# An attention kernel: the weighing of two quarters in one place, and waits at the quarter that needs them

## The chip, the cores and the metric

The kernel runs on one core of one Trainium2 chip. The metric is the device time of the whole program in microseconds. A core has a matrix engine (TensorE, "PE" in the profile; its weight loads are "PEld"), VectorE ("DVE"), ScalarE ("ACT"), GpSimd ("POOL") and SyncE ("SP"), which here only issues DMA. Each runs its own instructions in order and waits for the others by semaphores.

## What is computed

A transformer block over 2 batches of 2048 tokens with 512 features, 16 heads of 32, followed by a rotation of the features. The part that the change touches is the attention:

```python
scores = einsum('bhqd,bhkd->bhqk', q / sqrt(32), k) + attention_bias   # bias: 2 x 16 x 2048 x 2048
scores = where(src_mask, -inf, scores)
probs = softmax(scores, axis=-1)
ctx = einsum('bhqk,bhkd->bhqd', probs, v)
```

Ahead of it stand a layer norm with modulation and the projections to q, k and v; behind it the output projection, a second layer norm, a GELU feed-forward of 2048 and the rotation. All is in 32-bit floats; the bias alone is 512 MB that is read once.

## The kernel before

Three phases run one after the other: projections, attention (`phase_b`), and output projection with feed-forward. Attention goes over 64 trips (a head and half of a batch's queries) of 8 tiles of 128 queries each, so 512 tiles. A tile is 128 queries by 2048 keys; its bias lies in one of the 8 slots of `ring`. Four tiles (`QT`) make a unit of 512 queries; 128 units in all, two to a trip, and `probT` has room for two.

A tile i passes the engines like this:

- SyncE loads the bias into `ring[j]` as soon as the tile 8 before it has been turned in full (line 543); GpSimd adds the mask's penalty to it (line 572).
- TensorE computes the scores in two halves of 1024 keys (`score`, c = 0 and 1, two matmuls of 512 keys each), and adds the penalty of the last 192 keys with one more matmul (line 721).
- VectorE adds scores and bias of each half, writes the sum back to the ring and keeps the running minimum of the negated sum (`add`, line 636). The second half starts from the minimum of the first (`low_part`), and so waits on VectorE's own counter `added` (line 631).
- ScalarE takes the exponential of the whole tile (line 668), in the next step.
- TensorE turns the tile two steps after its scores: four quarters (`turn`, n = 0 to 3), each of four transposes of 128x128 into one PSUM bank (line 749). There are three banks for this; `turn_bank` gives the quarters the banks 0, 1, 2, 0 in even tiles and 2, 1, 0, 2 in odd ones. So a quarter can be turned only when the one before it in that bank has been copied out.
- ScalarE copies quarters 0 and 1 to `probT` (line 678, counter `out_act`), VectorE quarters 2 and 3 (line 620, counter `out_dve`).
- TensorE weighs the values of a whole unit with `probT` (`weigh`, line 772): for each quarter four matmuls of 32 columns side by side, which sum in `bank_ctx` over the four quarters. The profile counts each of them twice, since it goes through the array in two passes.

The order of each engine within a step is written out by hand. TensorE: scores of half 0 and half 1, quarters 0 and 1, one quarter of the weighing, quarters 2 and 3. The four quarters of a unit's weighing thus fall to four steps in a row. The waits for free banks stand earlier than their quarters: the one for the exponential ahead of the last score matmul of half 0 and the one for quarter 2 of the tile before ahead of the last of half 1 (`free_before_turn`), others in the middle of a quarter (c = 2). VectorE: add 0, copy of quarter 3 of the tile three steps back, add 1, copy of quarter 2 of the tile two steps back. ScalarE: exponential, copies of quarters 0 and 1, in some steps a copy of `bank_ctx`.

Even and odd steps are those with even and odd j, the place of the tile in its trip.

## Time and profile before

| | |
|---|---|
| median of 3 runs | 3553.28 us (3551.06 to 3555.66) |
| the profiled execution | 3553.73 us, its span 3552.1 us |
| mean granted clock of TensorE | 0.984 |
| TensorE matmul busy | 3418.1 us, 96% |
| VectorE busy | 2482.1 us, 70% |
| GpSimd busy | 2074.7 us, 58% |
| ScalarE busy | 1885.3 us, 53% |
| memory traffic | 906.14 MB, 255 GB/s over the span |

The page cuts the span into 40 slices. In those of the attention phase TensorE, VectorE and DMA all stand at 9 tenths or more and ScalarE at 8; in the others TensorE alone does. A busy share is therefore to be read in the attention phase alone: there three engines are nearly full, and which of them sets the pace is seen only from the order in which they wait for each other. In the rows, an instruction's start is measured and the end of a matmul is modelled; matmuls overlap in the array, so the distance from start to start is what one costs. The count behind a row says how many like instructions it merges.

### The profile page before, as it was taken

How to read it: one execution, taken by the hardware profiler on the slowest of the kernel's cores; microseconds unless marked ns; L12 is line 12 of the kernel's file. 1: busy time of each engine (PE TensorE's matmuls, PEld its weight loads, DVE VectorE, ACT ScalarE, POOL GpSimd, SP SyncE). 2: the span in 40 equal slices, each digit the busy share in tenths (PEclk: the TensorE clock that was granted, in tenths of full speed). 3: DMA queues.
4: the chain of work that ended last, by engine and by line, in shares of the span. 5: the costliest groups of instructions: out<-in, count | busy, mean ns of one | idle time of the engine just before them, and what ended most of it. 6: DMA issues, size and time to landing. Idle time of an engine off the chain costs nothing. (4 is left out here: it accounts for less than half of the span.)

```text
span 3552.1 us, 61044 instructions
## 1 busy us (share of the span) xinstructions
PE 3418.1 (96%) x18338; PEld 1942.0 (55%) x18338; DVE 2482.1 (70%) x4177; ACT 1885.3 (53%) x2538; POOL 2074.7 (58%) x642
## 2 busy tenths in 40 slices
PE   8999799999999999999999999994899999999997
PEld 3444466666666666666666666662344444444443
DVE  5665599999999999999999999993334333343332
ACT  3222388888888888888888888883111111111110
POOL 0000599999899998999998999992202201210100
PEclk9999899999999999999999999997899999999999
DMA  8999999999999999999999999996302211220100
GB/s 290 336 338 340 363 360 348 351 345 345 397 350 349 350 345 365 380 350 346 347 349 385 360 349 347 347 349 207 89 8 63 71 28 43 71 56 15 47 12 12
DMA packets 290234, 906.14 MB, mean 255 GB/s; under 512 B 93344, under 2 KB 93344, under 8 KB 213408
## 3 DMA queue, kind: packets, MB, share of 16 engines
q1 hardware_dynamic: 237584, 803.04, 63.1%
q10 hardware_dynamic: 50064, 94.39, 7.6%
q0 software_dynamic: 2560, 8.39, 0.7%
q8 instruction: 13, 0.21, 0.0%
q14 instruction: 13, 0.11, 0.0%
HBM read 763.12 MB, written 142.61 MB: 255 GB/s over the span
## 5 line engine op out<-in xcount | busy, mean ns | idle before, releaser
L572 POOL TENSOR_TENSOR ring<-ring,penb 128x1856 f32<-128x1856 f32 x512 | 1904.3, 3752 | 503.9 <-DMA penb<-pen_scratch 417.1
L668 ACT ACTIVATE ring<-ring,low 128x2048 f32<-128x2048 f32 x512 | 1028.6, 2009 | 319.2 <-DVE low L636 319.2
L749 PEld LDWEIGHTS b_T<-ident,ring 128*128 128x128 f32 x8192 | 889.3, 141 | 431.1 <-DVE probT L620 427.8
L749 PE MATMUL b_T<-ident,ring 128*128 128x128 f32 x8192 | 1090.8, 276 | 3.7 <-DVE probT L620 3.7
L636 DVE CUSTOM_DVE_ANT_0 ring<-scores,ring 128x1024 f32<-128x1024 f32 x512 | 627.2, 1225 | 177.6 <-PE scores L715 153.8
L620 DVE COPY probT<-b_T 128x512 f32<-128x512 f32 x1024 | 702.3, 686 | 4.5 <-PE b_T L749 4.5
L636 DVE CUSTOM_DVE_ANT_0 ring<-scores,ring,low_part 128x1024 f32<-128x1024 f32 x512 | 652.8, 1275 | 0.4
L715 PE MATMUL scores<-keys,queries 128*128 (+1 forms) x2048 | 621.8, 425 | 21.3 <-DMA queries<-q_rows 16.9
L772 PE MATMUL bank_ctx<-probT,values 128*32 128x512 f32 x4096 | 544.9, 604 | 0.0
L678 ACT COPY probT<-b_T 128x512 f32<-128x512 f32 x1024 | 537.8, 575 | 2.0 <-PE b_T L749 2.0
L939 POOL TENSOR_TENSOR y_out<-rot_a,rot_b 128x512 f32<-128x512 f32 x32 | 40.5, 1266 | 787.3 <-DVE rot_b L1097 787.3
L991 ACT ACTIVATE gate<-c_up,b_scaled 128x512 f32<-128x512 f32 x128 | 87.9, 687 | 741.1 <-PE c_up L1148 741.0
L1148 PE MATMUL c_up<-hT,w 128*128 (+1 forms) x1024 | 460.8, 594 | 0.7 <-ACT hT L983 0.7
L1158 PE MATMUL c_acc<-w,hidden 128*128 128x512 f32 x1024 | 458.9, 592 | 0.0
L715 PEld LDWEIGHTS scores<-keys,queries 128*128 128x128 f32 x2048 | 347.1, 190 | 144.1 <-DVE probT L620 74.3
L1078 DVE SCALAR_TENSOR_TENSOR hidden<-c_up,b_col,gate 128x512 f32<-128x512 f32 x128 | 96.0, 750 | 396.2 <-ACT gate L991 377.6
L1158 PEld LDWEIGHTS c_acc<-w,hidden 128*128 128x128 f32 x1024 | 194.0, 190 | 241.5 <-issue 241.5
L1148 PEld LDWEIGHTS c_up<-hT,w 128*128 128x128 f32 x1024 | 191.3, 191 | 223.1 <-issue 222.1
L932 POOL TENSOR_TENSOR parts<-parts 128x1024 f32<-128x1024 f32 x30 | 70.8, 2360 | 161.4 <-DMA parts<-ctx_scratch 161.0
L1129 PE MATMUL c_fore<-wo,ctxT 128*128 128x512 f32 x256 | 117.3, 603 | 19.0 <-DVE ctxT L1031 19.0
L721 PE MATMUL scores<-penb,identb 128*128 128x192 bf16 x512 | 131.7, 257 | 0.0
L772 PEld LDWEIGHTS bank_ctx<-probT,values 128*32 128x32 f32 x4096 | 80.8, 108 | 86.9 <-issue 86.6
(102 smaller groups left out, 1738.9 us busy)
## 6 DMA issues: line engine op xcount, KB each, us to landing
ring<-in_fside_Bx16xSxS SPq DMA_DIRECT2D x512, 1024.0 KB, 7.5
keys<-k_rows SPq DMA_DIRECT2D x64, 1024.0 KB, 8.5
values<-v_heads ACTq DMA_DIRECT2D x128, 256.0 KB, 6.5
queries<-q_rows SPq DMA_DIRECT2D x128, 256.0 KB, 8.1
ctx_scratch<-ctxp ACTq DMA_DIRECT2D x128, 256.0 KB, 6.8
parts<-ctx_scratch SPq DMA_DIRECT2D x128, 256.0 KB, 4.9
k_rows<-part_hi SPq DMA_DIRECT2D x64, 256.0 KB, 3.3
k_rows<-part_lo SPq DMA_DIRECT2D x64, 256.0 KB, 3.6
```

The source lines that it names most:

```text
L572: nc.gpsimd.tensor_tensor(ring[:, j, 0:POOL_MASKED], ring[:, j, 0:POOL_MASKED], penb[:, j, 0:POOL_MASKED], ALU.add).then_inc(masked, 1)
L620: nc.vector.tensor_copy(probT[:, hh, QR * n:QR * (n + 1), q * P:(q + 1) * P], turn_bank(k, n)[:].rearrange("p (c q) -> p c q", c=QR)).then ...
L636: nc.vector.tensor_tensor_reduce(out=at, in0=scores[c][:], in1=at, scale=-1.0, scalar=low_part[:, j:j + 1] if c else -MASKED, op0=ALU.add, ...
L668: nc.scalar.activation(ring[:, k, :], ring[:, k, :], ACT.Exp, bias=low[:, k:k + 1], scale=-1.0, accum_out=column(sums_all, trip, k)).then_ ...
L678: nc.scalar.copy(probT[:, hh, QR * n:QR * (n + 1), q * P:(q + 1) * P], turn_bank(k, n)[:].rearrange("p (c q) -> p c q", c=QR)).then_inc(ou ...
L715: last = nc.tensor.matmul(scores[c][:, n * N:(n + 1) * N], queries[:, hh, q * P:(q + 1) * P], keys[:, bass.ds(it % 2, 1), c * CW + n * N:c ...
L721: last = nc.tensor.matmul(scores[c][:, CW - PE_MASKED:CW], identb[:], penb[:, j, POOL_MASKED:S], start=False, stop=True)
L749: last = nc.tensor.transpose(turn_bank(slot, n)[:, c * P:(c + 1) * P], ring[:, slot, at:at + P], ident[:])
L772: last = nc.tensor.matmul(bank_ctx[DH * c:DH * (c + 1), :], values[:, hh, QR * n + c, :], probT[:, hh, QR * n + c, :], start=(n == 0), sto ...
L1129: last = nc.tensor.matmul(fore[t % 2][:], ctxT[:, c, t * P:(t + 1) * P], wo[:, c, :], start=(c == 0), stop=(c == DB - 1))
L1148: last = nc.tensor.matmul(up[f % 2][:], w1[:, c, f * P:(f + 1) * P], hT[:, bass.ds(u % 2, 1), c, :].rearrange("p o n -> p (o n)"), start=( ...
L1158: last = nc.tensor.matmul(acc[t][:], hidden[:, k % 4, t * P:(t + 1) * P], w2[:, k, :], start=(k == 0), stop=(k == FB - 1))
```

## The change

Four things are changed, all in `phase_b`:

- `weigh` runs in even steps alone, between the third and the fourth quarter, and takes two quarters of the unit (0 and 1 where j is 2 or 6, 2 and 3 where j is 0 or 4), sixteen passes in place of eight.
- TensorE's waits stand directly ahead of what needs them: exponential and the copy of the tile before's quarter 2 at quarter 0, that of quarter 1 at quarter 1, that of quarter 3 at quarter 2, that of this tile's quarter 0 at quarter 3; those of the weighing at the weighing.
- VectorE copies quarter 3 in the same step as quarter 2, so that its order is add 0, add 1, copy of quarter 2, copy of quarter 3.
- ScalarE's step is cut into functions; the order of its instructions stays.

```diff
--- before.py
+++ after.py
@@ -608,9 +608,9 @@
         def _(dve):
             nc.vector.tensor_copy(identb[:], ident[:]).then_inc(identb_ready, 1)
 
-            def copy_quarter(it, j, n, lag):
-
-                t, k = it * R + j - lag, (j - lag) % R
+            def copy_quarter(it, j, n):
+
+                t, k = it * R + j - 2, (j - 2) % R
                 hh, q = k // QT, k % QT
                 if live(t, NT):
                     dve.wait_ge(turned, TURNED0 + t * 4 + n + 1)
@@ -640,9 +640,9 @@
 
             def step(it, j):
                 add(it, j, 0)
-                copy_quarter(it, j, 3, 3)
                 add(it, j, 1)
-                copy_quarter(it, j, 2, 2)
+                copy_quarter(it, j, 2)
+                copy_quarter(it, j, 3)
 
             trips(dve, step)
 
@@ -657,7 +657,8 @@
             load_values(0, 0)
             load_values(0, 1)
 
-            def step(it, j):
+            def exponentials(it, j):
+
                 i = it * R + j
                 if live(i - 1, NT):
                     k, trip = (j - 1) % R, it if j else it - 1
@@ -667,16 +668,23 @@
                         nc.scalar.copy(low_all[:, bass.ds(trip, 1), :].rearrange("p o n -> p (o n)"), low[:]).then_inc(low_kept, 1)
                     nc.scalar.activation(ring[:, k, :], ring[:, k, :], ACT.Exp, bias=low[:, k:k + 1], scale=-1.0,
                                          accum_out=column(sums_all, trip, k)).then_inc(exp_done, 1)
+
+            def copy_quarter(it, j, n):
+                i = it * R + j
                 if live(i - 2, NT):
                     k = (j - 2) % R
                     hh, q = k // QT, k % QT
-                    for n in (0, 1):
-                        act.wait_ge(turned, TURNED0 + (i - 2) * 4 + n + 1)
-                        if q == 0 and n == 0:
-
-                            act.wait_ge(pv_done, PV0 - 1 + (it * 2 if j == 2 else it * 2 + 1))
-                        nc.scalar.copy(probT[:, hh, QR * n:QR * (n + 1), q * P:(q + 1) * P],
-                                       turn_bank(k, n)[:].rearrange("p (c q) -> p c q", c=QR)).then_inc(out_act, 1)
+                    act.wait_ge(turned, TURNED0 + (i - 2) * 4 + n + 1)
+                    if q == 0 and n == 0:
+
+                        act.wait_ge(pv_done, PV0 - 1 + (it * 2 if j == 2 else it * 2 + 1))
+                    nc.scalar.copy(probT[:, hh, QR * n:QR * (n + 1), q * P:(q + 1) * P],
+                                   turn_bank(k, n)[:].rearrange("p (c q) -> p c q", c=QR)).then_inc(out_act, 1)
+
+            def step(it, j):
+                exponentials(it, j)
+                copy_quarter(it, j, 0)
+                copy_quarter(it, j, 1)
                 unit, hh = closing(it, j), 0 if j < QT else 1
                 if j % QT == 1 and live(unit, UNITS):
                     act.wait_ge(pv_done, PV0 + unit + 1)
@@ -709,8 +717,6 @@
                         pe.wait_ge(q_in[hh], it * 16 + 16)
                     need(pe, added, i * CH + c - 1)
                 for n in range(CW // N):
-                    if n == CW // N - 1:
-                        free_before_turn(it, j, c)
                     if live(i, NT):
                         last = nc.tensor.matmul(scores[c][:, n * N:(n + 1) * N], queries[:, hh, q * P:(q + 1) * P],
                                                 keys[:, bass.ds(it % 2, 1), c * CW + n * N:c * CW + (n + 1) * N].rearrange("p o n -> p (o n)"),
@@ -722,66 +728,57 @@
                                                 start=False, stop=True)
                     last.then_inc(scored, 1)
 
-            def free_before_turn(it, j, c):
-
-                t = it * R + j - 2
+            def turn(it, j, n):
+
+                t, slot = it * R + j - 2, (j - 2) % R
                 if live(t, NT):
-                    if c == 0:
+                    if n == 0:
                         pe.wait_ge(exp_done, t + 1)
-                    else:
                         need(pe, out_dve, t * 2 - 1)
-
-            def turn(it, j, n):
-
-                t, slot = it * R + j - 2, (j - 2) % R
-                if n == 2 and live(t, NT):
-                    need(pe, out_dve, t * 2)
-                for c in range(QR):
-                    if c == 2:
-                        if n == 0 and live(t, NT):
-                            need(pe, out_act, t * 2)
-                        if n == 1:
-                            copied_before_weigh(it, j)
-                        if n == 2 and live(t, NT):
-                            pe.wait_ge(out_act, t * 2 + 1)
-                    if live(t, NT):
+                    if n == 1:
+                        need(pe, out_act, t * 2)
+                    if n == 2:
+                        need(pe, out_dve, t * 2)
+                    if n == 3:
+                        pe.wait_ge(out_act, t * 2 + 1)
+                    for c in range(QR):
                         at = (QR * n + c) * P
                         last = nc.tensor.transpose(turn_bank(slot, n)[:, c * P:(c + 1) * P], ring[:, slot, at:at + P], ident[:])
-                if live(t, NT):
                     last.then_inc(turned, 1)
 
             def weighed(it, j):
+
                 unit = it * 2 - 2 if j < 2 else it * 2 - 1 if j < 6 else it * 2
-                return (j - 2) % QT, unit, 1 if 2 <= j < 6 else 0
+                return unit, 1 if 2 <= j < 6 else 0, 0 if j % QT == 2 else 2
 
             def copied_before_weigh(it, j):
 
-                n, unit, hh = weighed(it, j)
+                unit, hh, n = weighed(it, j)
                 if live(unit, UNITS):
-                    pe.wait_ge(out_act if n < 2 else out_dve, (unit * QT + QT - 1) * 2 + n % 2 + 1)
+                    if n == 0:
+                        pe.wait_ge(v_in[hh], it * 16 if j == 2 else it * 16 + 16)
+                        need(pe, ctx_copied, unit)
+                    pe.wait_ge(out_act if n == 0 else out_dve, (unit * QT + QT) * 2)
 
             def weigh(it, j):
 
-
-                n, unit, hh = weighed(it, j)
-                if live(unit, UNITS) and n == 0:
-                    pe.wait_ge(v_in[hh], it * 16 if j == 2 else it * 16 + 16)
-                    need(pe, ctx_copied, unit)
-                for c in range(4):
-                    if live(unit, UNITS):
-                        last = nc.tensor.matmul(bank_ctx[DH * c:DH * (c + 1), :], values[:, hh, QR * n + c, :],
-                                                probT[:, hh, QR * n + c, :], start=(n == 0), stop=(n == 3))
-                if live(unit, UNITS) and n == 3:
+                copied_before_weigh(it, j)
+                unit, hh, first = weighed(it, j)
+                for n in (first, first + 1):
+                    for c in range(4):
+                        if live(unit, UNITS):
+                            last = nc.tensor.matmul(bank_ctx[DH * c:DH * (c + 1), :], values[:, hh, QR * n + c, :],
+                                                    probT[:, hh, QR * n + c, :], start=(n == 0), stop=(n == 3))
+                if live(unit, UNITS) and first == 2:
                     last.then_inc(pv_done, 1)
 
             def step(it, j):
                 score(it, j, 0)
                 score(it, j, 1)
-                turn(it, j, 0)
-                turn(it, j, 1)
-                weigh(it, j)
-                turn(it, j, 2)
-                turn(it, j, 3)
+                for n in range(4):
+                    if n == 3 and j % 2 == 0:
+                        weigh(it, j)
+                    turn(it, j, n)
 
             trips(pe, step)
```

## Rows read from the trace of the kernel before

**Rows 1.** Page, part 1: busy us (share of the span) and instructions.

```profile
PE 3418.1 (96%) x18338; PEld 1942.0 (55%) x18338; DVE 2482.1 (70%) x4177; ACT 1885.3 (53%) x2538; POOL 2074.7 (58%) x642
```

**Rows 2.** Windows, one stretch of the attention phase; columns named in line one.

```profile
core 0: us, PE busy (x) PEld busy (x) DVE busy (x) ACT busy (x) POOL busy (x), PEclk, DMA share, GB/s
...
1500.00:1900.00 400.00, 400.00 (x2938) 258.25 (x2935) 368.40 (x607) 324.92 (x443) 378.38 (x102) 1.00 0.95 347
```

**Rows 3.** Timeline of TensorE, a step: start us, us, engine line op tiles xcount.

```profile
1501.05 0.27 PE L749 MATMUL b_T<-ident,ring 128*128 128x128 f32 x1
1501.08 1.20 PE L715 MATMUL scores<-keys,queries 128*128 x4
...
1502.13 0.26 PE L721 MATMUL scores<-penb,identb 128*128 128x192 bf16 x1
...
1502.22 1.04 PE L749 MATMUL b_T<-ident,ring 128*128 128x128 f32 x8
...
1503.18 1.06 PE L772 MATMUL bank_ctx<-probT,values 128*32 128x512 f32 x8
...
1504.18 1.09 PE L749 MATMUL b_T<-ident,ring 128*128 128x128 f32 x8
...
1505.03 1.27 PE L715 MATMUL scores<-keys,queries 128*128 x4
```

**Rows 4.** Timeline of TensorE in cuts that split the groups of rows 3.

```profile
1501.40 0.40 PE L715 MATMUL scores<-keys,queries 128*128 x1
...
1503.64 0.61 PE L772 MATMUL bank_ctx<-probT,values 128*32 128x512 f32 x4
...
1504.35 0.38 PE L749 MATMUL b_T<-ident,ring 128*128 128x128 f32 x2
```

**Rows 5.** Timeline of VectorE, the same step.

```profile
1502.03 1.23 DVE L636 CUSTOM_DVE_ANT_0 ring<-scores,ring 128x1024 f32<-128x1024 f32 x1 [0.30 <-PE scores L715]
...
1503.18 0.69 DVE L620 COPY probT<-b_T 128x512 f32<-128x512 f32 x1
1503.78 1.27 DVE L636 CUSTOM_DVE_ANT_0 ring<-scores,ring,low_part 128x1024 f32<-128x1024 f32 x1
...
1504.98 0.69 DVE L620 COPY probT<-b_T 128x512 f32<-128x512 f32 x1
```

**Rows 6.** Timeline, a copy of VectorE and TensorE's weight load that waits for it.

```profile
1501.04 0.69 DVE L620 COPY probT<-b_T 128x512 f32<-128x512 f32 x1
...
1501.78 0.19 PEld L715 LDWEIGHTS scores<-keys,queries 128*128 128x128 f32 x1 [0.20 <-DVE probT L620]
```

**Rows 7.** Timeline of GpSimd, four tiles in a row.

```profile
1600.29 14.90 POOL L572 TENSOR_TENSOR ring<-ring,penb 128x1856 f32<-128x1856 f32 x4 [0.19 <-DMA ring<-in_fside_Bx16xSxS]
```

**Rows 8.** Timeline of VectorE in the phase's first steps, without copies between adds.

```profile
397.76 1.28 DVE L636 CUSTOM_DVE_ANT_0 ring<-scores,ring,low_part 128x1024 f32<-128x1024 f32 x1
...
402.62 1.23 DVE L636 CUSTOM_DVE_ANT_0 ring<-scores,ring 128x1024 f32<-128x1024 f32 x1 [3.56 <-issue]
...
403.98 1.28 DVE L636 CUSTOM_DVE_ANT_0 ring<-scores,ring,low_part 128x1024 f32<-128x1024 f32 x1
...
407.76 1.28 DVE L636 CUSTOM_DVE_ANT_0 ring<-scores,ring,low_part 128x1024 f32<-128x1024 f32 x1
...
408.97 0.69 DVE L620 COPY probT<-b_T 128x512 f32<-128x512 f32 x1
```

**Rows 9.** Timeline at the phase's end: two copies, then transposes behind a wait.

```profile
2421.96 1.28 DVE L620 COPY probT<-b_T 128x512 f32<-128x512 f32 x2
...
2422.76 0.31 PEld L749 LDWEIGHTS b_T<-ident,ring 128*128 128x128 f32 x3 [0.77 <-issue]
...
2422.93 0.49 PE L749 MATMUL b_T<-ident,ring 128*128 128x128 f32 x3
```

**Rows 10.** Timeline of ScalarE, the exponential of the same step.

```profile
1501.24 2.01 ACT L668 ACTIVATE ring<-ring,low 128x2048 f32<-128x2048 f32 x1 [0.89 <-DVE low L636]
```

**Rows 11.** Timeline of TensorE in the first steps: scores that wait for add 1.

```profile
399.11 1.22 PE L715 MATMUL scores<-keys,queries 128*128 128x512 f32 x2 [0.20 <-DVE low L636]
```

More of the change, by code:

```diff
@@ L723, in score @@
                     last.then_inc(scored, 1)
-            def free_before_turn(it, j, c):
-                t = it * R + j - 2
-                if live(t, NT):
-                    if c == 0:
-                        pe.wait_ge(exp_done, t + 1)
-                    else:
-                        need(pe, out_dve, t * 2 - 1)
             def turn(it, j, n):
                 t, slot = it * R + j - 2, (j - 2) % R
-                if n == 2 and live(t, NT):
-                    need(pe, out_dve, t * 2)
-                for c in range(QR):
-                    if c == 2:
-                        if n == 0 and live(t, NT):
-                            need(pe, out_act, t * 2)
-                        if n == 1:
-                            copied_before_weigh(it, j)
-                        if n == 2 and live(t, NT):
-                            pe.wait_ge(out_act, t * 2 + 1)
-                    if live(t, NT):
+                if live(t, NT):
+                    if n == 0:
+                        pe.wait_ge(exp_done, t + 1)
+                        need(pe, out_dve, t * 2 - 1)
+                    if n == 1:
[5 more added lines that the diff above has]
+                    for c in range(QR):
                         at = (QR * n + c) * P
                         last = nc.tensor.transpose(turn_bank(slot, n)[:, c * P:(c + 1) * P], ring[:, slot, at:at + P], ident[:])
-                if live(t, NT):
                     last.then_inc(turned, 1)
```

## The prediction

> **What bounds the kernel now.** I read the page's busy shares first: TensorE 96%, VectorE 70% [rows 1]. These are means over three phases; the change touches only the attention phase of 512 steps. So next the busy time of a stretch inside it [rows 2]: in 400 us TensorE is busy all of the time at granted clock 1.00, and it ran 2938 matmuls. A step has 29 (4 scores, 1 mask, 16 transposes, 8 of weighing), so a step lasts 400 / (2938 / 29) = 3.948 us. Times 512 that is 2021 us of the 3552.1.
>
> The timeline of TensorE shows what the 3.95 us are [rows 3, 4]. Scores start at 1501.08, the mask at 1502.13, eight transposes at 1502.22, weighing at 1503.18, eight transposes at 1504.18, the next scores at 1505.03. Transposes are 0.109 us apart (from 1504.35 to 1505.03 are six of them and 0.03 us of hand-over). From the last transpose to the weighing are 0.96 - 7 x 0.109 = 0.20 us, where the next transpose would have come after 0.11. A weighing pass (four matmuls side by side) lasts 1503.64 - 1503.18 = 0.46 us; the second one is followed by the first transpose after 0.60 (1504.35 - 0.11 - 1503.64). So entering and leaving the weighing costs 0.09 + 0.14 = 0.23 to 0.24 us, once a step. Nothing of it is idle beyond that: TensorE is the bound.
>
> VectorE is close behind [rows 5]: add 0 at 1502.03, copy 1.15 later, add 1 another 0.60 later, copy another 1.20 later, then 0.69 of copy and 0.30 of waiting for the scores. Its work alone is 1.15 + 0.60 + 1.20 + 0.60 = 3.55 us a step. The weight load of the last score matmul already waits for the copy that started at 1501.04 [rows 6]; the matmul itself is late by at most 0.02. GpSimd needs 14.90 / 4 = 3.72 a tile and waits for DMA in between [rows 7]. So the step could not fall below 3.72 in any case.
>
> **The change part by part.**
>
> *Weighing two quarters at once, in even steps.* The matmuls stay. One entry and one exit of two go: TensorE's own work for two steps falls from 7.90 to 7.66 us. But an odd step is now 3.95 - 1.15 = 2.80 us of it and an even one 4.86. A weighing of two quarters lasts 0.20 + 3 x 0.46 + 0.60 = 2.18 us from the last transpose of the third quarter to the first of the fourth [rows 3, 4].
>
> *VectorE: the copy between the adds goes behind them.* Add 1 takes its running minimum from add 0 and waits for its completion. Now a copy covers that wait: add 0 to copy 1.15, copy to add 0.60 [rows 5]. Where no copy lies between them, in the first steps of the phase, add 1 starts 403.98 - 402.62 = 1.36 us after add 0, and the copy behind it 1.21 later [rows 8]. So the wait costs 0.21 us a step once its cover is gone. Two copies in a row are 0.60 apart: the row of two at 2421.96 is 1.28 long, one is 0.69 [rows 9, 5]. VectorE's work rises from 3.55 to 1.36 + 1.21 + 0.60 + 0.60 = 3.77 us. Alone that still fits under 3.95.
>
> The Trainium skill speaks against this price: "VectorE: DVE Perf Modes", section "The DRAIN you can't avoid", has a semaphore between chained operations cost nothing extra. The row shows 0.21 us for this pair, a form with an accumulator.
>
> *The fourth quarter's copy moves a step earlier, ahead of the next add 0.* Queued behind it on VectorE is now everything of the next step. In an even step the fourth quarter is turned only after the two-quarter weighing, so VectorE stands at this copy while TensorE weighs, and can't start add 0 the sooner for anything, since the next scores come behind the same transposes.
>
> *The waits stand at the quarter.* Satisfied waits cost nothing: the transposes with one inside a quarter are as far apart as the others. The wait for the third quarter's copy leaves the last score matmul (gain at most 0.02) and goes to the first transpose. What it costs there if it is late is shown at the phase's end [rows 9]: copies start at 2421.96, the second transpose behind the wait at 2422.93, so the first in effect at 2422.82, 0.86 after the start of the first copy. The lower bound is the older place: weight load 1501.78 after copy 1501.04 = 0.74 [rows 6]. I take 0.86, which is this very pair of waits with this very instruction behind it.
>
> *ScalarE* keeps its order (exponential, copies of quarters 0 and 1); it stands idle for 0.89 us ahead of each exponential [rows 10], so I cost it at nothing. If that cover went, the fourth quarter of odd steps would be late, and there TensorE has the half microsecond of slack that the sum below gives it. SyncE's loads of the ring still hang on the fourth quarter and GpSimd gets more time a tile than now, not less: nothing. The second weighing, and with it the release of the context bank, ends a step earlier than now, which nobody waits for.
>
> **The sum.** What decides is a round trip of two steps, from add 0 of an odd step to add 0 of the next odd step:
> - add 0 to add 1, 1.36; add 1 to the third quarter's copy, 1.21 [rows 8];
> - this copy to the first transpose of the even step, 0.86 [rows 9];
> - twelve transposes, start of first to start of last, 11 x 0.109 = 1.20; weighing 0.20 + 1.38 + 0.60 = 2.18; fourth quarter 3 x 0.109 = 0.33 [rows 3, 4];
> - last transpose at 1501.05 to second score matmul at 1501.40, 0.35; that to add 0 at 1502.03, 0.63 [rows 3 to 5].
> Together 8.12 us, 4.06 a step; with the passes at 0.454 and the other figures unrounded 8.09, or 4.045. All of it is in series: the copy can't start before add 1 is done, the quarter not before the copy, since they share a bank. TensorE needs 7.66 and VectorE 7.54 for the same two steps, so about 0.45 us of each pair is idle on TensorE. It would show in even steps, ahead of the second pair of scores, which waits for add 1 (0.4), and ahead of the first quarter (0.1).
>
> The change is then 4.045 - 3.948 = +0.097 us a step, times 512 = +50 us. To the profiled execution (span 3552.1, 3553.7 in all) that makes 3603; the median of the runs is 0.4 below it, so 3603 again; I say 3602, since what VectorE now and then waits for GpSimd can only shrink at a slower pace.
>
> Bounds: if the copy hands over in 0.74, the trip is 7.97; it can't be much less, as the second pair of scores needs add 1 as well: add 1 at 397.76 [rows 8], scores at 399.11 [rows 11], 1.35, then 0.23 + 0.26 + 0.09 to the first transpose, 1.93 against my 2.07. That is 3.985, or 3573. Upwards: each further quarter of the even step that finds its wait late, or just met, loads weights unhidden, about 0.06 from the load at 2422.76 to the transpose [rows 9]; two of them make 8.21, 4.105, or 3634.
>
> **The rivals.**
>
> *The forecast*, +0.097 a step: 0.70, from 3573 to 3625.
>
> *The round trip is hidden and TensorE stays the bound (faster).* Place: the hand-over at the first quarter of even steps. Price: two steps take TensorE's 7.66, 3.83 each, -0.118 x 512 = -60: 3493. It decides if the trip is 7.66 or less, so if 0.43 us of the sum above isn't in series. For it: TensorE is the bound today by a hair only, and entering and leaving is real work saved. Against it: every term has a row of its own, and the two terms that the change brings (0.21 of the self-wait, 0.92 of a second weighing behind the third quarter) can't lie elsewhere. 0.10.
>
> *The self-wait is free.* The same trip with 1.15 in place of 1.36 is 7.88, 3.94 a step, which is the present pace: 3550. For it would speak only that the rows of the first steps belong to a start in which VectorE waited for other things; but nothing in them is between the two adds. 0.05. It is the result that the skill's rule named above would give.
>
> *Further late waits (slower still).* TensorE's sequencer stands at the first quarter's wait and behind it has to compute and pass the waits of two quarters and three of the weighing. Place: the first to third quarter of even steps. Price: 0.12 us or more of a pair, 3625 to 3650. It decides if these take longer than the 1.3 us of twelve transposes. 0.12.
>
> *Nothing happens*, as the two costs and the gain cancel, or the instructions end up in the order of now: 3554, 0.03.
>
> **How the numbers follow.** The likeliest is 3602. From 3565 to 3640 lie nearly all of the forecast's 0.70 and most of the slower rival, together about 0.8; the faster rival, the two near 3550 and the far end are left out. A measurement of this kernel tells apart about 0.2%, 7 us. Faster by more: 0.11 (the faster rival and a little of the third). Within: 0.08. Slower: 0.81.
>
> **What would show it.** The two steps should differ: on TensorE first transpose to first transpose about 4.8 us from an even step to an odd one, 3.3 from an odd to an even. Add 0 to add 1 should be 1.36 in every step. VectorE should wait about 0.5 us for the fourth quarter in even steps and hardly elsewhere. The weighing should be a block of 16 matmuls and about 1.9 us, its entry and exit as now. The transposes of even steps should be released by VectorE's copy. If instead TensorE is busy without a gap and a pair of steps lasts 7.66, the sum was wrong in the hand-over; if add 0 to add 1 is 1.15, in the self-wait; if a pair is over 8.2, waits cost TensorE more than the end of the phase shows. A fall of the granted clock from 1.00 would break all of it; at this busy share I see none in the rows.

## The result and the profile after

The changed kernel takes 3589.95 us (median of 4 runs, 3588.65 to 3592.43), the kernel before 3552.17 beside it. The ratio is 1.0106, 95% interval 1.0088 to 1.0123: 38 us slower, where 50 were forecast. The profiled execution's span is 3587.0 us, against 3552.1. Line numbers have moved: the transposes are now L746 (L749 before), the scores L721 (L715), the mask L727 (L721), the weighing L770 (L772), ScalarE's copies L681 (L678) and its exponential L669 (L668); VectorE's lines are the same.

The page of the changed kernel, busy shares and VectorE's groups (busy us, mean ns | idle before, releaser), answers to [rows 1]:

```profile
PE 3413.2 (95%) x18338; PEld 1963.3 (55%) x18338; DVE 2517.2 (70%) x4177; ACT 1903.4 (53%) x2538; POOL 2073.9 (58%) x642
...
L620 DVE COPY probT<-b_T 128x512 f32<-128x512 f32 x1024 | 680.9, 686 | 92.1 <-PE b_T L746 92.1
...
L636 DVE CUSTOM_DVE_ANT_0 ring<-scores,ring,low_part 128x1024 f32<-128x1024 f32 x512 | 657.4, 1284 | 76.0 <-DVE low_part L636 11.0
```

TensorE's busy share went down by one point only. The groups say more: VectorE's copies, which waited for TensorE for 4.5 us in all, now do for 92.1 us, and add 1 has 76.0 us of idle time before it, part of it put down to VectorE itself (`low_part`). The stretch that answers to [rows 2]:

```profile
core 0: us, PE busy (x) PEld busy (x) DVE busy (x) ACT busy (x) POOL busy (x), PEclk, DMA share, GB/s
1500.00:1900.00 400.00, 391.74 (x2879) 256.64 (x2877) 368.24 (x597) 322.01 (x435) 371.87 (x101) 1.00 0.88 342
```

2879 matmuls in 400 us are 400 / (2879 / 29) = 4.029 us a step, against 3.948. TensorE still reads as 98% busy, because the end of a matmul is modelled and covers much of the gap behind it. DMA fell from 0.95 to 0.88, and the granted clock is 1.00 in both, so the clock is no cause. A pair of steps on TensorE, answering to [rows 3] (steps with weighing begin their transposes at 1501.68 and 1509.73, the one without at 1506.48):

```profile
1501.68 1.50 PE L746 MATMUL b_T<-ident,ring 128*128 128x128 f32 x12
...
1506.48 1.93 PE L746 MATMUL b_T<-ident,ring 128*128 128x128 f32 x16
1508.17 0.71 PE L721 MATMUL scores<-keys,queries 128*128 x2
1509.04 0.73 PE L721 MATMUL scores<-keys,queries 128*128 x2 [0.16 <-DVE low L636]
1509.61 0.26 PE L727 MATMUL scores<-penb,identb 128*128 128x192 bf16 x1
1509.73 1.50 PE L746 MATMUL b_T<-ident,ring 128*128 128x128 f32 x12
1511.17 1.92 PE L770 MATMUL bank_ctx<-probT,values 128*32 128x512 f32 x16
1513.02 0.66 PE L746 MATMUL b_T<-ident,ring 128*128 128x128 f32 x4
1513.43 1.18 PE L721 MATMUL scores<-keys,queries 128*128 x4
```

and in cuts, as [rows 4]:

```profile
1509.87 0.38 PE L746 MATMUL b_T<-ident,ring 128*128 128x128 f32 x2
...
1512.48 0.61 PE L770 MATMUL bank_ctx<-probT,values 128*32 128x512 f32 x4
...
1513.19 0.38 PE L746 MATMUL b_T<-ident,ring 128*128 128x128 f32 x2
```

From first transpose to first transpose are 4.80 and 3.25 us in turn. Where the distance from the scores' start to the mask was 1.05 us, it is 1.44 in the step with weighing (1508.17 to 1509.61): the second pair of scores waits for add 1. VectorE in the same pair, answering to [rows 5] and [rows 8]:

```profile
1506.31 1.22 DVE L636 CUSTOM_DVE_ANT_0 ring<-scores,ring 128x1024 f32<-128x1024 f32 x1
...
1507.69 1.28 DVE L636 CUSTOM_DVE_ANT_0 ring<-scores,ring,low_part 128x1024 f32<-128x1024 f32 x1
...
1508.90 1.28 DVE L620 COPY probT<-b_T 128x512 f32<-128x512 f32 x2
...
1512.68 0.69 DVE L620 COPY probT<-b_T 128x512 f32<-128x512 f32 x1
1513.72 0.69 DVE L620 COPY probT<-b_T 128x512 f32<-128x512 f32 x1 [0.35 <-PE b_T L746]
1514.38 1.22 DVE L636 CUSTOM_DVE_ANT_0 ring<-scores,ring 128x1024 f32<-128x1024 f32 x1
```

Add 0 to add 1 is 1.38 us, and the fourth quarter's copy at 1513.72 comes after 0.35 us of idle time behind the one at 1512.68, released by the transposes that stand behind the weighing (0.5 was forecast). From add 0 at 1506.31 to add 0 at 1514.38 the pair takes 8.07 us; most pairs take 8.05 to 8.06.

From the first mask (the matmul with the penalty, one a step) to the last the 512 steps take 2061.8 us in this trace and 2022.2 in that of before, 39.6 more; the loss lies in the attention phase.

### The profile page after: what moved, and what is told of

Its sections match the earlier page's. It is cut to its first block and busy times, and to the rows that moved or that the text cites. A ratio compares the mean times of both kernels' runs of the same rounds, so it can differ in the third digit from the quotient of the medians.

```text
span 3587.0 us, 61239 instructions
## 1 busy us (share of the span) xinstructions
PE 3413.2 (95%) x18338; PEld 1963.3 (55%) x18338; DVE 2517.2 (70%) x4177; ACT 1903.4 (53%) x2538; POOL 2073.9 (58%) x642
## 5 line engine op out<-in xcount | busy, mean ns | idle before, releaser
L669 ACT ACTIVATE ring<-ring,low 128x2048 f32<-128x2048 f32 x512 | 1028.2, 2008 | 306.0 <-DVE low L636 306.0
L746 PE MATMUL b_T<-ident,ring 128*128 128x128 f32 x8192 | 1047.0, 276 | 2.1 <-DVE probT L620 1.3
L746 PEld LDWEIGHTS b_T<-ident,ring 128*128 128x128 f32 x8192 | 884.7, 141 | 226.6 <-ACT probT L681 213.4
L620 DVE COPY probT<-b_T 128x512 f32<-128x512 f32 x1024 | 680.9, 686 | 92.1 <-PE b_T L746 92.1
L721 PE MATMUL scores<-keys,queries 128*128 (+1 forms) x2048 | 660.8, 429 | 63.0 <-DVE low L636 29.8
L681 ACT COPY probT<-b_T 128x512 f32<-128x512 f32 x1024 | 544.5, 582 | 53.4 <-PE b_T L746 53.4
L770 PE MATMUL bank_ctx<-probT,values 128*32 128x512 f32 x4096 | 492.3, 598 | 0.3 <-issue 0.3
L721 PEld LDWEIGHTS scores<-keys,queries 128*128 128x128 f32 x2048 | 330.0, 190 | 197.7 <-DVE low L636 114.8
L770 PEld LDWEIGHTS bank_ctx<-probT,values 128*32 128x32 f32 x4096 | 107.1, 109 | 196.7 <-issue 196.7
L727 PE MATMUL scores<-penb,identb 128*128 128x192 bf16 x512 | 131.7, 257 | 0.0
```

The lines of the kernel that those rows point to most:

```text
L620: nc.vector.tensor_copy(probT[:, hh, QR * n:QR * (n + 1), q * P:(q + 1) * P], turn_bank(k, n)[:].rearrange("p (c q) -> p c q", c=QR)).then ...
L669: nc.scalar.activation(ring[:, k, :], ring[:, k, :], ACT.Exp, bias=low[:, k:k + 1], scale=-1.0, accum_out=column(sums_all, trip, k)).then_ ...
L681: nc.scalar.copy(probT[:, hh, QR * n:QR * (n + 1), q * P:(q + 1) * P], turn_bank(k, n)[:].rearrange("p (c q) -> p c q", c=QR)).then_inc(ou ...
L721: last = nc.tensor.matmul(scores[c][:, n * N:(n + 1) * N], queries[:, hh, q * P:(q + 1) * P], keys[:, bass.ds(it % 2, 1), c * CW + n * N:c ...
L727: last = nc.tensor.matmul(scores[c][:, CW - PE_MASKED:CW], identb[:], penb[:, j, POOL_MASKED:S], start=False, stop=True)
L746: last = nc.tensor.transpose(turn_bank(slot, n)[:, c * P:(c + 1) * P], ring[:, slot, at:at + P], ident[:])
```

## The experiments

The theory is the round trip of the prediction. Against it stand two others: that waits placed directly at a quarter cost TensorE its early weight loads (rival A in the expectations), and that VectorE's greater work is what bounds the kernel (rival B). All times below are medians; the kernel before took 3551.1 to 3553.6 us beside them. Intervals are those of the ratio to it.

### One part of the change taken away or done alone

**Pairing undone.** One quarter, `first = (j - 2) % QT`, is weighed in each step, between the second and the third turned quarter, with its own waits; the rest is as changed.

```diff
-                for n in (first, first + 1):
+                for n in (first,):
...
-                    if n == 3 and j % 2 == 0:
+                    if n == 2:
                         weigh(it, j)
```

> The changed kernel with the pairing undone: one quarter weighed in each step, between the second and the third; waits at the quarter and VectorE's order as changed. Theory: a step fits a step, the hand-over has 0.1 us to spare, TensorE alone sets the pace with 3.92 us, 3534 us, faster than the kernel before. Rival A: entries and exits of the weighing are back and the waits still stand at the quarter, slower than 3590, about 3650. Rival B: 3590.

Measured: 3538.67 us, ratio 0.9957 (0.9941 to 0.9974), 0.4% faster than the kernel before. The stretch from 1500 to 1900 us (columns as above):

```profile
1500.00:1900.00 400.00, 400.00 (x2962) 260.64 (x2958) 378.27 (x613) 327.77 (x447) 379.14 (x102) 1.00 0.95 351
```

Both new waits and new order of the copies stand in this kernel, and it is 15 us faster than the one before, not slower. Rivals A and B fall here, and the pairing is what costs. The run also puts the weighing back ahead of the third quarter; a single quarter weighed between the third and the fourth was not run, so that the number weighed and not the place decides rests on the sum.

**Waits alone.** The kernel before, with only `free_before_turn` and the other waits moved to their quarters, as in the change's `turn`.

```diff
-                    if n == CW // N - 1:
-                        free_before_turn(it, j, c)
...
+                    if n == 0:
+                        pe.wait_ge(exp_done, t + 1)
+                        need(pe, out_dve, t * 2 - 1)
```

> The kernel before with only TensorE's waits moved directly to their quarters and to the weighing. Theory: satisfied waits cost nothing, and the last score matmul no longer waits for VectorE's copy (0.02 a step): 3.92 to 3.95 a step, 3534 to 3552 us. Rival A: each wait at its quarter costs 0.06, slower than before, 3590 or more. Rival B: no change, 3552.

Measured: 3540.84 us, ratio 0.9964 (0.9950 to 0.9978).

```profile
1500.00:1900.00 400.00, 400.00 (x2958) 260.43 (x2956) 370.73 (x613) 327.79 (x447) 380.23 (x103) 1.00 0.96 351
```

**Copies alone.** The kernel before, with only VectorE's order changed.

```diff
                 add(it, j, 0)
-                copy_quarter(it, j, 3, 3)
                 add(it, j, 1)
-                copy_quarter(it, j, 2, 2)
+                copy_quarter(it, j, 2)
+                copy_quarter(it, j, 3)
```

> The kernel before with only VectorE's order changed: both adds, then both copies. Theory: add 0 to add 1 rises to 1.37 us and VectorE's work to 3.78 a step, but TensorE needs 3.92 and the round trip fits in it: 3.92 to 3.95 a step, 3534 to 3552 us. Rival B (VectorE's added work is what costs): 3590.

Measured: 3536.17 us, ratio 0.9957 (0.9940 to 0.9973).

```profile
1500.00:1900.00 400.00, 400.00 (x2960) 260.41 (x2959) 378.73 (x613) 328.33 (x447) 378.47 (x102) 1.00 0.95 352
```

VectorE's busy time in the stretch is 378.73 us with the copies at the end and 370.73 with the waits alone; the pace is the same to within a step of the count. Each part alone takes off what the early wait cost, and either is enough. Below that TensorE's own work bounds the step. Not all of that cost lay at VectorE's copy. In the kernel before, the step with the turn of the loop is longer, 4.02 us from mask to mask where the others take 3.92 to 3.96, and its last weight load for scores is late by issue:

```profile
1505.80 0.19 PEld L715 LDWEIGHTS scores<-keys,queries 128*128 128x128 f32 x1 [0.27 <-issue]
```

In the kernel with the waits alone all eight steps of a trip take 3.93. A trip is 0.21 us shorter there: 0.10 of it in the step of the turn, 0.11 in the other seven.

**Pairing alone.** The kernel before, with the changed `weigh` in even steps; waits and copies as before.

```diff
-                turn(it, j, 0)
-                turn(it, j, 1)
-                weigh(it, j)
-                turn(it, j, 2)
-                turn(it, j, 3)
+                for n in range(4):
+                    if n == 3 and j % 2 == 0:
+                        weigh(it, j)
+                    turn(it, j, n)
```

> The kernel before with only the pairing: two quarters weighed between third and fourth turned quarter of even steps; VectorE's order and the early waits as before. Theory: without VectorE's new order the pairing puts the fourth quarter's late copy into a line with every third quarter, as in the run with the copy between the adds: 3930 us or somewhat more. If the three parts were independent: waits alone took 12 off and copies alone 16, so pairing alone would be 3552 + 38 + 28 = 3618.

Measured: 3933.55 us, ratio 1.1074 (1.1054 to 1.1094). The parts are not independent. Had they been, this would be near 3618.

**The old copies in the changed kernel.** VectorE's step is put back: the fourth quarter is copied a step late, between the adds.

```diff
                 add(it, j, 0)
+                copy_quarter(it, j, 3, 3)
                 add(it, j, 1)
-                copy_quarter(it, j, 2)
-                copy_quarter(it, j, 3)
+                copy_quarter(it, j, 2, 2)
```

> The changed kernel with VectorE's old order: the fourth quarter's copy a step late, between the adds. The self-wait is covered again. Theory: the third quarter of a step now waits for the copy behind add 0 of the same step, and in the step behind a weighing this stands in line with it: by the same kind of sum 9.5 us a pair, 4.74 a step, about 3960 us. If covering the self-wait were what counts: 3.91 a step, 3532. Rival A: 3590.

Measured: 3931.34 us, ratio 1.1067 (1.1045 to 1.1089). VectorE, then TensorE, in a pair of steps:

```profile
1507.75 1.23 DVE L636 CUSTOM_DVE_ANT_0 ring<-scores,ring 128x1024 f32<-128x1024 f32 x1 [2.05 <-PE scores L721]
...
1508.90 0.69 DVE L620 COPY probT<-b_T 128x512 f32<-128x512 f32 x1
...
1509.64 1.09 PE L746 MATMUL b_T<-ident,ring 128*128 128x128 f32 x8 [0.69 <-DVE probT L620]
...
1513.32 0.66 PE L746 MATMUL b_T<-ident,ring 128*128 128x128 f32 x4 [0.69 <-DVE probT L620]
1513.91 1.92 PE L770 MATMUL bank_ctx<-probT,values 128*32 128x512 f32 x16
```

Add 0 at 1507.75 comes only after the weighing of the step before (2.05 us idle), the late copy follows at 1508.90, and only then can the third quarter be turned (1509.64, 0.69 us idle on that copy). The same stands at 1513.32 in the step with weighing. So VectorE's new order is what makes the pairing bearable, though it uncovers the self-wait.

**The early wait in the changed kernel.** Exponential and third quarter of the tile before are waited for ahead of the last score matmul of each half again (the exponential in the first, the quarter in the second).

```diff
+                    if n == CW // N - 1:
+                        free_before_turn(it, j, c)
...
-                    if n == 0:
-                        pe.wait_ge(exp_done, t + 1)
-                        need(pe, out_dve, t * 2 - 1)
```

> The changed kernel with the waits for the exponential and for the tile before's third quarter put back ahead of the last score matmul of either half. Theory: this wait lies on the round trip, and 0.24 + 0.09 us of matmuls now come behind it in place of ahead of it: 0.29 a pair (0.74 + 0.08 + 0.24 + 0.09 = 1.15 from copy to first transpose in place of 0.86), 8.35, 4.17 a step, about 3660 us. Rival A (a wait directly at the quarter costs more than an early one): faster than 3590. If the place doesn't matter: 3590.

Measured: 3673.71 us, ratio 1.0344 (1.0329 to 1.0360). VectorE's copy and TensorE in a step with weighing:

```profile
1495.13 1.28 DVE L620 COPY probT<-b_T 128x512 f32<-128x512 f32 x2
...
1495.87 0.19 PEld L723 LDWEIGHTS scores<-keys,queries 128*128 128x128 f32 x1 [0.42 <-DVE probT L620]
...
1496.21 0.26 PE L729 MATMUL scores<-penb,identb 128*128 128x192 bf16 x1
...
1496.30 1.47 PE L754 MATMUL b_T<-ident,ring 128*128 128x128 f32 x12
```

From the copy at 1495.13 the weight load of the last score matmul is 0.74 us away and the first transpose 1.17; 1.15 had been expected, and 0.86 are there with the direct wait. In the step behind the turn of the loop it is 1.26. Pairs last 8.37 us, where 8.35 were expected, and 8.45 with the turn in them. In the changed kernel the move of the waits is thus a gain of 84 us.

### Single terms of the round trip

**Self-wait.** Add 1 starts its minimum from a constant.

```diff
                     else:
-                        dve.wait_ge(added, i * CH + c)
                         if j == 0:
...
-                                                   scalar=low_part[:, j:j + 1] if c else -MASKED,
+                                                   scalar=-MASKED,
```

> The changed kernel in which add 1 takes its minimum from a constant and not from add 0, so that it need not wait for it; the minimum of the first half is left out of the softmax's shift. Theory: add 0 to add 1 falls from 1.37 to 1.15 us, once in the round trip, 7.83, so 3.914 a step and 3532 us. If the wait between the adds were free, or not on the path: 3590. Rival A: 3590. Rival B: VectorE's work falls to 3.55, at least as fast as the kernel before, 3552 or less.

Measured: 3530.62 us, ratio 0.9934 (0.9918 to 0.9951): 59 us less than the changed kernel.

```profile
1507.36 1.23 DVE L635 CUSTOM_DVE_ANT_0 ring<-scores,ring 128x1024 f32<-128x1024 f32 x1
...
1508.51 1.22 DVE L635 CUSTOM_DVE_ANT_0 ring<-scores,ring 128x1024 f32<-128x1024 f32 x1
...
1509.65 0.69 DVE L620 COPY probT<-b_T 128x512 f32<-128x512 f32 x1
```

Add 0 to add 1 is 1.15 us, and add 1 to the copy 1.14 in place of 1.21: this form, without a scalar from memory, is shorter too. Both lie on the trip, 0.23 + 0.07 = 0.30 of a pair: 0.15 a step, times 512 is 77 us. In this kernel a pair lasts 7.77 us, but 8.03 where the loop turns in it: 0.26 once in 64 trips is 17 us, and 77 - 17 is about the 59 measured. The run takes away the wait and the scalar from memory together. That the form alone does not delay its own start is seen in [rows 5]: behind a copy, with the wait already met, add 1 starts after 0.60 us, as one copy does behind another. So the 0.23 are put down to the wait.

**Hand-over, longer.** The first quarter of each tile waits for VectorE's next copy too.

```diff
-                        need(pe, out_dve, t * 2 - 1)
+                        need(pe, out_dve, t * 2)
```

> The changed kernel whose first quarters wait for VectorE's next copy too, which ends 0.60 us later. Theory: the link from VectorE to TensorE lies on the round trip of two steps, which becomes 8.05 + 0.60 = 8.65, 4.33 a step, 3743 us. If this hand-over isn't on the path: 3590 to 3610. Rival A, as no wait is added: 3590.

Measured: 3737.07 us, ratio 1.0520 (1.0499 to 1.0541). 0.60 us more on the link are 147 us more in all, 0.29 a step: the link is on the path, at its full price.

**Hand-over, taken away.** Even tiles take their banks in another order, so that their first quarter uses the bank that ScalarE freed and the second the one that VectorE copies last; the waits for these two banks change places with them.

```diff
-            return bankT[(0, 1, 2, 0)[n] if t % 2 == 0 else (2, 1, 0, 2)[n]]
+            return bankT[((0, 1, 2, 0), (2, 1, 0, 2), (1, 0, 2, 1), (2, 0, 1, 2))[t % 4][n]]
```

> The changed kernel with other banks: even tiles turn their first quarter into the bank that ScalarE freed long ago and their second into the one that VectorE copies last. Theory (a round trip of two steps, 8.05 us, with the hand-over from VectorE's copy to the first quarter of even steps as its link): this link goes, the next longest is add 1 to the second pair of scores, 1.35 + 0.47 + 0.09 = 1.91 in place of 1.21 + 0.86 = 2.07, so the trip is 7.90, 3.95 a step, about 3549 us. Rival A (the waits at the quarter as such cost TensorE its early weight loads): as many waits stand as before, 3590. Rival B (VectorE is the bound, since its work rose from 3.55 to 3.78 us a step): 3590.

Measured: 3579.80 us, ratio 1.0075 (1.0058 to 1.0092). Only 10 us came off of 41 expected. VectorE's add 1 and copy, then TensorE:

```profile
1510.43 1.28 DVE L636 CUSTOM_DVE_ANT_0 ring<-scores,ring,low_part 128x1024 f32<-128x1024 f32 x1
...
1511.64 1.28 DVE L620 COPY probT<-b_T 128x512 f32<-128x512 f32 x2
...
1511.78 0.73 PE L721 MATMUL scores<-keys,queries 128*128 x2 [0.15 <-DVE low L636]
1512.35 0.26 PE L727 MATMUL scores<-penb,identb 128*128 128x192 bf16 x1
1512.44 1.47 PE L747 MATMUL b_T<-ident,ring 128*128 128x128 f32 x12
```

The transposes at 1512.44 no longer wait for the copy at 1511.64. They stand right behind the mask, and this behind scores that wait for add 1: 1510.43 to 1511.78 is the 1.35 us that the prediction had, but from there to the mask are 0.57 us and not 0.47, since the weight load behind the wait is not hidden. In all 2.01 us from add 1 to the first transpose, where the way over the copy is 2.07. The two ways run side by side with 0.05 us between them. The theory stands, its bound for the second way was 0.10 too low.

**Both together.** The edits of the last run and of the one on the self-wait in one kernel.

> The changed kernel with the other banks and with add 1 independent of add 0; the minimum of the first half is left out of the softmax's shift. Theory, corrected by the trace of the run with other banks: the way over the second pair of scores (2.02 us from add 1 to the first transpose) runs beside the way over the copy (2.07) and is only 0.05 shorter, so banks give 0.05 us a pair and the free self-wait 0.22: 8.06 - 0.27 = 7.79, 3.89 a step, about 3519 us. If the bank change's small gain had another cause than a parallel way, such as TensorE's own work: 3530, as without it. If both were worth what was first expected of them (0.16 and 0.22): 3.84 a step, 3493.

Measured: 3523.41 us, ratio 0.9919 (0.9906 to 0.9933), 4 us above what was expected. The interval overlaps that of the self-wait's run. The traces are clearer: most pairs last 7.71 us in place of 7.77, and from first mask to last the steps take 1992.7 us in place of 2003.1. So the banks are worth 0.05 us a pair here too, and not 0.16.

**Weighing between the halves of the scores.** The weighing of even steps stands behind the first half's scores.

```diff
                 score(it, j, 0)
+                if j % 2 == 0:
+                    weigh(it, j)
                 score(it, j, 1)
```

> The changed kernel with the pair weighed between the two halves of the scores of even steps. Theory: the wait of the second half for add 1 is covered by weighing, but all four quarters of the even step then come behind it, and VectorE's add 1 too: by the same sum 7.97 us a pair, 3.984 a step, 3568 us. If any place that keeps TensorE busy would do: 3.81 a step, 3480. Rivals A and B: 3590.

Measured: 3633.68 us, ratio 1.0228 (1.0211 to 1.0245), 66 us above what was expected. VectorE, ScalarE and TensorE in a pair of steps, and VectorE again:

```profile
1502.21 1.28 DVE L636 CUSTOM_DVE_ANT_0 ring<-scores,ring,low_part 128x1024 f32<-128x1024 f32 x1 [0.85 <-PE scores L727]
...
1503.62 2.01 ACT L669 ACTIVATE ring<-ring,low 128x2048 f32<-128x2048 f32 x1
...
1505.62 0.56 ACT L681 COPY probT<-b_T 128x512 f32<-128x512 f32 x1
...
1506.24 0.66 PE L746 MATMUL b_T<-ident,ring 128*128 128x128 f32 x4 [0.16 <-ACT probT L681]
1506.65 0.71 PE L721 MATMUL scores<-keys,queries 128*128 x2
1507.41 1.92 PE L770 MATMUL bank_ctx<-probT,values 128*32 128x512 f32 x16
1509.27 0.73 PE L721 MATMUL scores<-keys,queries 128*128 x2
...
1510.33 1.28 DVE L636 CUSTOM_DVE_ANT_0 ring<-scores,ring,low_part 128x1024 f32<-128x1024 f32 x1 [0.71 <-PE scores L727]
```

Another round trip has taken over. The late second half makes add 1 late (1502.21), the exponential waits for it (1503.62), ScalarE's copy of the first quarter for the exponential (1505.62), and the fourth quarter of the odd step, in the same bank, for that copy (1506.24, 0.16 us idle on it). Then come the next scores, weighing, scores, and add 1 at 1510.33: 8.12 us. The expectation of 7.97 names no link over ScalarE; it is the engine that the prediction cost at nothing, with this very quarter as the one that would be late if its cover went. Of the four pairs of a trip two last 8.05 and 8.12 us. One lasts 8.27; in the one that was read, ScalarE issues the store of `ctxp` (its copy of `bank_ctx`) just ahead of the exponential, which starts 1.68 us after add 1 in place of 1.41. The one with the loop's turn lasts 8.48. The mean is 8.23 us, 4.115 a step.

### The turn of the loop

In the kernel with other banks and two minima, pairs of steps last 7.71 us, but one in four 8.03. Masks and scores on TensorE:

```profile
1567.15 0.26 PE L726 MATMUL scores<-penb,identb 128*128 128x192 bf16 x1
...
1574.86 0.26 PE L726 MATMUL scores<-penb,identb 128*128 128x192 bf16 x1
...
1581.85 1.20 PE L720 MATMUL scores<-keys,queries 128*128 x4 [0.19 <-issue]
1582.89 0.26 PE L726 MATMUL scores<-penb,identb 128*128 128x192 bf16 x1
```

1567.15 to 1574.86 is 7.71 and from there to 1582.89 are 8.03; in this pair lie the loop's turn and scores that wait for nothing but issue. The last run unrolls TensorE's loop three times.

```diff
-            trips(pe, step)
+            with pe.Fori(0, (TRIPS - 1) // 3) as third:
+                for part in range(3):
+                    for j in range(R):
+                        step(third * 3 + (part + 1), j)
```

> The kernel with other banks and two minima (the minimum of the first half left out of the softmax's shift), and TensorE's loop unrolled: three trips of eight steps in one turn of the loop, so that 42 of 63 turns go. In its trace a pair of steps lasts 7.71 us, but 8.03 with the turn of the loop in it: TensorE's sequencer stands at the wait of the last quarter until just before it, and then needs 0.84 us for the turn and the next trip's waits, of which the branch shows about 0.37. Theory: the turn costs 0.3 us each time, 42 of them 11 to 13 us: about 3511. If the next trip's waits and registers are what is late and not the branch: 3523, as before.

Measured: 3511.92 us, ratio 0.9887 (0.9870 to 0.9903). Masks around the same place of the trip, without a branch:

```profile
1568.33 0.26 PE L726 MATMUL scores<-penb,identb 128*128 128x192 bf16 x1
...
1576.12 0.26 PE L726 MATMUL scores<-penb,identb 128*128 128x192 bf16 x1
```

7.79 us, where a turn gives 8.03: a turn costs 0.24, and 42 fewer of them are 10 us of the 11.5 measured (from first mask to last the two traces differ by 9.7). The other 0.08 of the difference to 7.71 stay without a turn, so the next trip's waits and registers, the expectation's other reading, may have a small part. This is the fastest kernel of the study, 1.1% faster than the one before. With it goes that the shift of the softmax no longer is the row's minimum over all keys; for rows whose halves differ much more than those of this input, the exponential could overflow.

## Why the prediction was right, point by point

**The bound.** Right. TensorE alone set the pace before, with VectorE's copy just late enough to touch the last score matmul. The prediction priced this at 0.02 us a step; the kernels without it run at 3.92 to 3.93 us a step against 3.952, and are 13 to 16 us faster. What it lacked is that about half of this lies in the one step of eight in which the loop turns.

**Pairing.** Right in direction and mechanism: 0.24 us of TensorE's work saved, but 0.9 of a second weighing moved into the trip. This is the term that was most too large. From the last transpose to the fourth quarter the sum had 2.18 us; measured are 0.20 + (1513.19 - 0.11 - 1511.17) = 2.11. Three passes last 1512.48 - 1511.17 = 1.31, where the sum took 0.46 for each: the first is as long as before, the later ones take 0.43.

**Self-wait.** Right: 1.36 forecast from the first steps, 1.38 measured in odd and 1.37 in even steps; 59 us when taken away. The Trainium skill ("VectorE: DVE Perf Modes", section "The DRAIN you can't avoid") has a semaphore between chained operations cost nothing extra, from a measurement of plain copies. Here it costs 0.23 us for an addition with an accumulator that starts from the last one's: the measurement decides.

**Hand-over.** 0.86 forecast from the phase's end. Measured: copy at 1508.90, second transpose at 1509.87, so 1509.87 - 0.11 - 1508.90 = 0.86. The lower bound of the prediction, the way over the second pair of scores, was priced 1.93; it is 2.01 to 2.02, because its weight load comes late. It decides what a repair can bring: 0.05 and not 0.16 us a pair.

**Waits.** Satisfied ones cost nothing, as forecast (every step is 3.93 us in the kernels with the waits alone and with the pairing undone). What the forecast lacked: a wait that is met late, just ahead of the loop's turn, costs the sequencer its lead. In the changed kernel it is hidden under the wait for add 1 but for 0.02 us a trip; in the faster kernels it is 0.25 to 0.32.

**The fourth quarter's copy.** The prediction took the new order of the copies as a cost of 0.21 us and nothing else. In the changed kernel that is so; in the kernel before TensorE covers it, and the new order alone gains 16 us. It did not say that with the pairing and the old order the kernel would be at 3930: of the change's parts this one saves the other.

**The sum.** 8.12 in round figures and 8.09 unrounded, against 8.05 to 8.06 for most pairs. 4.045 - 3.948 = 0.097 a step was forecast; 4.031 - 3.952 = 0.079 is the difference of the two traces over 432 steps. That is 9 of the 12 us by which the forecast was high. The weighing's later passes alone are 0.05 of a pair, 13 us; the self-wait was 0.015 too small and takes 4 of it back; the count of matmuls in a stretch had given the base 0.004 too low. Outside the 512 steps the profiled execution was some 5 us shorter than that of before, 4 of it behind the last mask, a stretch that takes 1129 to 1135 us in the traces of this study without any change to it.

**The rivals.** That the trip would be hidden and TensorE stay the bound needed 0.43 us less. All that the kernel with both edits (self-wait and bank) takes out of it is 0.35 of a pair. Further late waits in the even step did not show. What I said of the release of even steps' transposes is true by 0.05 us only; ahead of the first quarter TensorE idles for about that, where 0.1 was forecast.

## What to carry to other kernels

Work that is moved from every step into every second one saves its fixed cost only if each pair still fits; before merging, write out the round trip through the engine that is second busiest, with the merged piece inside it, and do it again when the piece moves: at another place the trip went over ScalarE. Where two engines pace each other, look for a place in the trace where an operation runs without its present cover (a loop's first and last steps): the price of the wait is there before the change is made. And test the parts in pairs as well as singly: here two parts that gain 13 and 16 us alone and one that costs 382 alone make a kernel that is 38 us slower.

## What was not expected of the hardware

Behind a wait that is met late, the weight load isn't hidden: with score matmuls of 512 columns this adds 0.10 us (0.57 in place of 0.47 from the first of a pair to the mask), with transposes 0.03 (0.14 in place of 0.11). Of four weighing passes in a row the first takes 0.45 us and the second and third 0.43 each. An addition that takes its starting value from memory lasts 1.21 us to the next operation and one with a constant 1.14. And what a turn of TensorE's loop costs depends on the waits around it: nothing in the kernel with the waits alone (3.93 us in every step), 0.10 us in the kernel before, and 0.24 us in the one with other banks and two minima, where a late wait stands directly before it.
